# First join: the residual add on GpSimd and one step more of lag; attention: both normalisings of the rows on GpSimd

## What is computed

```python
x = ln(x + rglru_3_layers(x))            # the last step of it is an rmsnorm with a weight
x = ln(x + moe_8_experts_top1(x))
x = ln(x + attention(x))                 # 16 heads; attention ends with (y - mean) / sqrt(var + 1e-3) * gamma + beta
x = ln(x + moe_16_experts_top4(x))
```

## Time and profile before

| | |
|---|---|
| median of 3 runs | 1974.94 us (1974.58 to 1975.36) |
| profiled execution, its own time | 1975.52 us |
| its span, first to last instruction | 1973.8 us |
| busy: PE, DVE, ACT, POOL | 1650.0, 1166.6, 1102.8, 612.8 us |
| mean granted TensorE clock | 0.915 |
| first join, about | 375 to 442 us |
| attention's main loop, about | 870 to 1268 us |

### The profile page before, as it was taken

The page is one execution under the profiler, slowest core; times in us unless marked ns, Lnnn a source line. Parts: engine busy times, 40 slices in busy tenths (PEclk is TensorE's granted clock), DMA queues, the critical chain, the costliest instruction groups (busy, mean ns, idle before and its releaser), DMA issues. The chain is left out here.

```text
span 1973.8 us, 33223 instructions
## 1 busy us (share of the span) xinstructions
PE 1650.0 (84%) x9891; PEld 1114.9 (56%) x9892; DVE 1166.6 (59%) x1942; ACT 1102.8 (56%) x2288; POOL 612.8 (31%) x562
## 2 busy tenths in 40 slices
PE   4999998461599689999999999924999999999990
PEld 1433333260499556444444444522899999999990
DVE  6999997478411164458999999268233333333324
ACT  6888987440133234138888888714455555555554
POOL 0000000000266231211222222110567777777750
PEclk9999999685699889989999999965899999999995
DMA  5000000124122296503334333177344444444417
GB/s 176 1 0 0 0 0 0 49 85 167 33 68 60 66 329 235 87 14 81 77 96 100 99 95 97 40 253 248 61 70 73 67 70 71 67 67 68 70 21 255
DMA packets 145736, 173.68 MB, mean 88 GB/s; under 512 B 29139, under 2 KB 110430, under 8 KB 145504
## 3 DMA queue, kind: packets, MB, share of 16 engines
q1 hardware_dynamic: 104160, 128.29, 21.3%
q0 software_dynamic: 33248, 43.71, 12.5%
q10 hardware_dynamic: 8224, 0.39, 0.2%
HBM read 111.50 MB, written 66.19 MB: 90 GB/s over the span
## 5 line engine op out<-in xcount | busy, mean ns | idle before, releaser
L1312 PEld LDWEIGHTS f_ht_ps<-f_XT,f_WS 128*128 128x128 f32 x2912 | 358.0, 195 | 15.8 <-DVE f_WS L1405 2.6
L1312 PE MATMUL f_ht_ps<-f_XT,f_WS 128*128 128x128 f32 x2912 | 361.8, 278 | 3.0 <-ACT f_XT L1353 3.0
L1320 PE MATMUL f_y_ps<-W,f_HT 128*128 x1456 | 344.1, 379 | 0.0
L2128 DVE TENSOR_REDUCE att_MX<-att_s_ps 128x2 f32<-128x1024 f32 x256 | 304.8, 1215 | 57.6 <-PE att_s_ps L1888 57.5
L1278 POOL DMA_INDIRECT moe<-f_Y,TOK x182 | 276.6, 1520 | 184.8 <-ACT f_Y L1378 122.1
L2093 ACT ACTIVATE att_PT<-att_st_ps 128x512 f32<-128x512 f32 x512 | 278.7, 595 | 53.7 <-PE att_st_ps L1913 46.2
L1320 PEld LDWEIGHTS f_y_ps<-W,f_HT 128*128 128x128 f32 x1456 | 262.8, 190 | 28.3
L1405 DVE COPY f_WS<-W 128x1024 f32 x182 | 133.7, 735 | 209.0 <-PE f_ht_ps L1312 128.0
L1269 POOL DMA_INDIRECT XG<-x,TOK x182 | 191.8, 1054 | 196.1 <-issue 125.9
L1413 DVE TENSOR_TENSOR f_Y<-f_y_ps,f_B 128x256 f32<-128x256 f32 x143 | 60.7, 425 | 292.4 <-PE f_y_ps L1320 292.4
L303 PE MATMUL rec_ring<-rec_XC,rec_W 128*128 128x512 f32 x384 | 181.7, 627 | 51.2 <-DVE rec_XC L353 21.6
(11 more groups left out here) (273 smaller groups left out, 2195.9 us busy)
## 6 DMA issues: line engine op xcount, KB each, us to landing
W<-in_w SPq DMA_DIRECT2D x48, 512.0 KB, 10.0
att_Q<-qk_pairs SPq DMA_DIRECT2D x192, 64.0 KB, 2.8
att_K<-qk_pairs SPq DMA_DIRECT2D x192, 64.0 KB, 2.9
qk_pairs<-prj_HI SPq DMA_DIRECT2D x16, 512.0 KB, 3.8
qk_pairs<-prj_LO SPq DMA_DIRECT2D x16, 512.0 KB, 5.1
hidden<-in_xT SPq DMA_DIRECT2D x8, 512.0 KB, 8.0
x<-n_Y SPq DMA_DIRECT2D x8, 512.0 KB, 3.0
prj_X<-x SPq DMA_DIRECT2D x8, 512.0 KB, 8.8
```

The source lines that it names most:

```text
L1312: mm = nc.tensor.matmul(ht_ps[r % 2][:, f * P:(f + 1) * P], WS[r % 2][:, at:at + P], XT[r % 2][:, c], start=(c == 0), stop=(c == DC - 1))
L1320: mm = nc.tensor.matmul(y_ps[r % 2][:], HT[r % 2][:, f], W2[:, bass.ds(e * W_EXPERT + f * D, D)], start=(f == 0), stop=(f == FC - 1))
L2128: nc.vector.tensor_reduce(MX[n % 2][:, qc, :, p], s_ps[m % 2][:], AX.X, ALU.max).then_inc(s_mx, 1)
```

## The change

In the first join VectorE's `add` is taken apart: `y_scale` (the scaling) and `z_moments` (statistics and aggregates) stay, the add of the residual rows is done by GpSimd, and the steps are spread over one group more. In attention the first normalising of batches 0 to 6 and the second of batches 0 to 5 go from ScalarE to GpSimd, as `tensor_scalar` with multiply and add, all four tiles at once behind the send of the maxima. The constants for ScalarE's slots go.

```diff
-    LAG = 2 if scaled_on_act else 3
+    LAG = 2 if scaled_on_act else 4
...
             st.clear_old(pool)
+            for q in range(GROUPS if rms_w is not None else 0):
+                k = q % N
+                if q >= len(rows):
+                    pool.wait_ge(s_x[k], loads * (q // N + 1))
+                elif q == 0:
+                    pool.wait_ge(rows_loaded, 16 * len(rows))
+                pool.wait_ge(s_y, QT * (q + 1))
+                nc.gpsimd.tensor_tensor(Y[k][:], X[k][:], Y[k][:], ALU.add).then_inc(s_sum, 1)
...
-                if 0 <= step - 1 < GROUPS:
-                    second(step - 1)
+                if 0 <= step - 2 < GROUPS:
+                    second(step - 2)
...
+            def y_scale(q):
...
+                dve.wait_ge(s_rstd1, q + 1)
+                for j in range(QT):
+                    n = QT // 2 * q + j // 2
+                    nc.vector.scalar_tensor_tensor(out=Y[k][:, j], in0=y_ps[n % QT][:, (j % 2) * D:(j % 2 + 1) * D],
+                                                   scalar=rstd1[:, k, j], in1=WB[:], op0=ALU.mult, op1=ALU.mult).then_inc(s_y, 1)
+
+            def z_moments(q):
+                dve.wait_ge(s_sum, q + 1)
+                moments(Y[q % N], stats, mv, q, s_mv)
...
-            for step in range(0 if scaled_on_act else GROUPS + 6):
+            for step in range(0 if scaled_on_act else GROUPS + 7):
                 if 0 <= step - 1 < GROUPS:
-                    add(step - 1)
+                    y_scale(step - 1)
                 if 0 <= step - 2 < GROUPS:
-                    normalise(step - 2)
-                if plus is not None and 0 <= step - 3 < GROUPS:
-                    next_residual(step - 3)
-                if router is not None and 0 <= step - 6 < GROUPS:
-                    copy_logits(step - 6)
+                    z_moments(step - 2)
+                if 0 <= step - 3 < GROUPS:
+                    normalise(step - 3)
+                if router is not None and 0 <= step - 7 < GROUPS:
+                    copy_logits(step - 7)
...
-Y_MOMENTS, Y_ROOT, Y_SHIFT, Y_NORM = KC, KC + 2, KC + 3, KC + 4
-Z_STATS, Z_MOMENTS, Z_ROOT, Z_SHIFT, Z_NORM = 18, 22, 24, 25, 26
+Y_MOMENTS, Y_ROOT, Y_SHIFT = KC, KC + 2, KC + 3
+Z_STATS, Z_MOMENTS, Z_ROOT, Z_SHIFT = 18, 22, 24, 25
...
+            def y_normalise(b):
+                pool.wait_ge(s_yshift, b + 1)
+                for j in range(KC):
+                    nc.gpsimd.tensor_scalar(rows_of(b)[:, j], rows_of(b)[:, j], yrstd[:, b, j], yshift[:, b, j],
+                                            ALU.mult, ALU.add).then_inc(s_yn, 1)
+
+            def z_normalise(b):
...
             for n in range(NGROUPS + 3):
                 if n < NGROUPS:
                     stack_maxima(n)
+                if n % PER == 0 and n >= 2 * PER:
+                    y_normalise(n // PER - 2)
+                if n % PER == 2 and n >= 2 * PER + 2 and n < NGROUPS:
+                    z_normalise(n // PER - 2)
                 if n >= 3:
                     add(n - 3)
...
             def join_step(b, s):
                 if s == Y_ROOT:
                     y_root(b)
-                if Y_NORM <= s < Y_NORM + KC:
-                    y_normalise(b, s - Y_NORM)
                 if s == Z_ROOT:
                     z_root(b)
-                if Z_NORM <= s < Z_NORM + KC:
-                    z_normalise(b, s - Z_NORM)
```

More of the change, by code:

```diff
@@ L707, in minus @@
                 return nc.vector.scalar_tensor_tensor(out=out, in0=mean, scalar=-1.0, in1=scale, op0=ALU.mult, op1=ALU.mult)
+            def y_scale(q):
+                k = q % N
+                if q >= N:
+                    dve.wait_ge(s_rstd, q - N + 1)
+                    dve.wait_ge(s_st[k], 16 * (q // N))
+                    if transposed:
+                        dve.wait_ge(s_zt, DC * (q - N + 1))
+                dve.wait_ge(s_rstd1, q + 1)
[6 more added lines that the diff above has]
+                moments(Y[q % N], stats, mv, q, s_mv)
             def add(q):
                 k = q % N
[L711 to L714, removed]
+                dve.wait_ge(s_x[k], loads * (q // N + 1))
                 if q >= N:
                     dve.wait_ge(s_rstd, q - N + 1)
[L717 to L727, removed]
                 if affine is not None:
@@ L1860, in residual @@
                 nc.gpsimd.tensor_tensor(rows_of(b), rows_of(b), X[b % XS][:], ALU.add).then_inc(s_sum, 1)
+            def y_normalise(b):
[4 more added lines that the diff above has]
+            def z_normalise(b):
+                pool.wait_ge(s_zshift, b + 1)
+                for j in range(KC):
+                    nc.gpsimd.tensor_scalar(rows_of(b)[:, j], rows_of(b)[:, j], zrstd[:, b, j], zshift[:, b, j],
+                                            ALU.mult, ALU.add).then_inc(s_z, 1)
             for k in range(2, STACKS):
```

## The result

The changed kernel takes **1959.49 us** (median of 5 runs, 1958.58 to 1964.03) against 1974.94: a ratio of 0.9923, 95% interval 0.9912 to 0.9934, 15.4 us less, where 10.2 were forecast. It is half a microsecond under the low end of the range. The profiled execution has a span of 1957.8 us.

What follows compares the result with a forecast made beforehand. VectorE was taken to set the pace in the first join, TensorE in attention's main loop. 5.7 us from the join plus 4.5 from attention, 10.2 off 1975.5, gave 1964.7 us off the median; range 1960.0 to 1971.5.

Steps and rivals of the forecast that it cites:

- Rival C: First join: normalising isn't held by GpSimd's add, steps of 4.82, gain 9.0 us, 1961.4 in all; chance 0.05.
- rival B: First join: TensorE's clock at half holds up a step, the join gains only 3.0 us, 1967.4 in all; chance 0.10.
- Normalising stands for 0.65, and runs 1.38: the step is 5.5 us: First join: VectorE's normalising waits 0.65 us for GpSimd's add, so a step falls from 6.03 to 5.5 us.
- I take 0.4 for TensorE's tail: End of the first join: TensorE has one group more behind it, costing 0.4 us of the 6.1 gained.
- I take 0: First join: scaling 1 meeting GpSimd's first add costs nothing, where the bounds were 0 and 1.7 us once.
- 0.10: Attention, group of 11.97: two normalisings leaving ScalarE gain 0.10 us a batch.
- 0.42: Attention, group of 12.83: TensorE's 0.42 us wait behind ScalarE's exponential is gained in each batch.
- 0.25: Attention, group of 12.12: four normalisings leaving ScalarE gain 0.25 us a batch.
- The second stays: Attention, group of 12.83: TensorE's 0.41 us wait behind a VectorE subtraction, slow beside GpSimd's add, remains.
- VectorE's own: Attention: the group of 12.46 is set by VectorE's load, busy 12.36 us, and stays as long.
- Rival A: Attention: ScalarE was never in the way, so only the first join gains, 1969.2 us in all; chance 0.12.
- rival D: Attention: GpSimd is slow at scale-and-shift, beyond 1.1 us an instruction; at 2.39 the kernel slows to 1994 us; chance 0.07.

Runs made afterwards that it cites:

- the kernel with halves: The changed kernel with GpSimd's first-join adds each cut in two of 128x512, each half waiting for its own two scalings; 1955.94 us, ratio 0.9897.
- the kernel with pieces: The changed kernel with GpSimd's multiply by gamma and residual add in attention each cut into four of 128x256; 1953.88 us, ratio 0.9889.
- first_norm_only: The changed kernel with attention's second normalisings of batches 0 to 5 back on ScalarE; 1963.23 us, ratio 0.9933.
- attn_only: Attention as in the changed kernel, the first join as in the kernel before; 1972.71 us, ratio 0.9978.
- vector_adds_spread: The changed kernel with the first join's eight residual adds back on VectorE, the wider spread of the steps kept; 1965.89 us (one run).

## Why the prediction missed, step by step

**The mechanism of the join was right, two of its terms were too dear.** The add left VectorE, normalising was the only thing held, the adds took the 2.35 us of the earlier trace rows, and nothing waited for GpSimd but the first moments, 0.16 us. Rival C (not held) and rival B (clock) both fell: past 405 us, where they came twice before, TensorE's half-clock products came once.

- *"Normalising stands for 0.65, and runs 1.38: the step is 5.5 us"* is the first step that failed. I laid durations end to end. They overlap: in the earlier trace rows a scaling takes 1.65, but in the changed kernel statistics that don't wait for it start 1.57 behind its start, and the four held normalisings run 1.92, not 2.03. The earlier trace rows already showed the second: the normalising there ended 0.14 us behind the add, although four in a row take 1.38 and one about a quarter of that. The step is 5.19. Over six steps that is 1.9 us.
- *"I take 0.4 for TensorE's tail"* is the second. The tail is 1.6 us shorter, not 0.4 longer: 2.0 us. I had read the earlier trace rows as the price of a half clock and had not asked where the kernel before pays it. It pays it a second time at 430.86, in the tail, for a wait that the spreading takes away. The kernel that only spreads has the shorter tail too, which shows it.
- 5.7 + 1.9 + 2.0 = 9.6; measured 9.4.
- The bound for rival C was short in its own terms: with steps of 4.82 the schedule gives 6.1 + 6 x 0.68 = 10.2, less 0.4 for the tail 9.8, not 9.0. With it the low end of the range would have been 1959.5, right at the measured time.
- *"I take 0"* for the scaling that meets the first add held: the scaling of 386.67 ran inside the adds of 386.11 to 390.77 and took 1.66. By the Trainium skill (SBUF — State Buffer, Who interferes with whom), an instruction with one input in SBUF outside the two-port modes doesn't contend; the traces agree, here and in the kernel with halves, where every scaling has an add beside it.

**Attention: 4.5 forecast, 4.2 by the change.** The six batches gave 0.61 each, 3.7 us (0.77 each forecast); the group of the last send gave 0.3 (12.82 to 12.53), and what lies behind it 0.3, so the seventh normalising brought 0.6 and not 0.9. Of the three terms of 0.77, *0.10* for the group of 11.97 was wrong, it didn't move in any kernel; *0.42* measured 0.33, as 0.49 less 0.17 for the dearer meeting, which no term had; *0.25* measured 0.27. That term was right in cause and near in size; what failed beside it is *"The second stays"*: the meeting stayed, but another instruction was held in it. Of the group of 12.46, *"VectorE's own"*, 0.45 was not its own, as the kernel with pieces shows; it stayed all the same. Rival A falls by that (its "VectorE is busy 11.2 to 12.4" should have read 11.0 to 12.4), and rival D by 546 ns, half of its deciding point: GpSimd's gap of 4.39 us had room for 2.16. The further 1.8 us in attention of the profiled execution lie ahead of the third group, with no changed work in them, and are not in the second execution.

**What no step had: the experts' block, 1.3 us.** TensorE's clock, table by stretch, where the first experts' products start; before, then after:

```profile
520.00:525.00 5.00, 4.09 (x18) 3.72 (x19) 0.00 (x0) 0.37 (x1) 3.86 (x4) 0.50 0.35 92
525.00:530.00 5.00, 4.39 (x21) 4.01 (x21) 0.69 (x1) 0.86 (x2) 2.14 (x3) 0.50 0.27 78
530.00:535.00 5.00, 5.00 (x34) 4.69 (x33) 1.39 (x2) 2.19 (x5) 1.29 (x1) 0.96 0.00 0
```
```profile
514.00:519.00 5.00, 4.27 (x19) 3.93 (x20) 0.69 (x1) 0.86 (x2) 3.98 (x4) 0.52 0.38 100
519.00:524.00 5.00, 5.00 (x38) 4.79 (x39) 0.69 (x1) 1.33 (x3) 1.01 (x1) 1.00 0.20 54
```

Before, some 10 us of products ran at 1.2 GHz until the clock was granted in full, after it some 5. It repeats: 240.3 us in three executions with the join of before, 238.3 to 239.2 in nine with a spread join, and once 241.3 (`first_norm_only`). The clock goes with it: counted from the block's first constant, it was granted in full from about 84 us on in these nine, and from about 88 in the other four, `first_norm_only` among them. So the length goes by the clock, and a spread join isn't enough for the earlier one. What decides when the clock comes back is left open, and whether the change causes it is not shown.

The sum for the medians: 9.4 + 4.2 + 1.3 = 14.9 of 15.4 us. That it closes so well is partly luck, since blocks without changed work differ by up to 2 us between executions.

## What to carry to other kernels

Work that moves to GpSimd should be put in pieces when VectorE has instructions that a GpSimd operation holds: the price of a meeting was the rest of the operation less 0.14 to 0.26 us (2.36 left cost 2.21, 0.80 cost 0.54, 0.27 cost 0.13, 0.17 nothing). A quarter of the size made a batch 1.1 us shorter although GpSimd worked 0.4 longer for each whole, but part of that was a new order of the two engines, so look after such a change at what now meets what. When a group takes longer than its engines' work, look into the group before it for a held instruction; a busy engine may be working off a debt. And price the drain behind a loop from its own rows: a half clock there cost its full 1.6 us, while the same in the loop (416.40) cost nothing.

## What the runs showed of the hardware

- GpSimd's multiply and add with two scalars a partition over 128x256 in fp32 takes 546 ns, its two-input operations of that size 726 to 732.
- Four GpSimd operations of 128x256 take 2.80 us, one of 128x1024 2.37; two of 128x512 take 2.51.
- Some VectorE instructions that meet a GpSimd operation with two inputs in SBUF stand until it is nearly or wholly over: the rounding took 2.39 us beside 2.37, against 0.18 alone, the subtraction 2.23, and normalising beside the add lost 0.54. Others run on: four statistics took 1.39 to 1.41 us, aggregates 0.38, and scalings 1.65 or 1.66, beside an add or not.
- The meeting in attention has three outcomes with the same code. The rounding is held (groups of 12.5 us), or the subtraction behind it (12.33), or neither, in one batch of six of `attn_only` and of `vector_adds_spread`: a group of 11.86 or 11.87, and behind it one of 11.99. Then GpSimd is the one that waits, 0.43 us behind the multiply instead of 0.14, after which its add starts in the middle of the subtraction, which takes its 0.18. The last outcome, in attention alone, VectorE and GpSimd:

```profile
1067.88 0.18 DVE L2146 CAST att_MS<-att_MX 128x16 fp32r<-128x16 f32 x1
1068.09 0.18 DVE L2147 TENSOR_TENSOR att_MS<-att_MX,att_MS 128x16 fp32r<-128x16 f32 x1
```
```profile
1065.35 2.38 POOL L1857 TENSOR_TENSOR att_OUT<-att_OUT,att_WB 128x1024 f32<-128x1024 f32 x1
1068.16 2.37 POOL L1860 TENSOR_TENSOR att_OUT<-att_OUT,att_X 128x1024 f32<-128x1024 f32 x1 [0.43 <-POOL att_OUT L1857]
```

In each of the three outcomes the rounding starts within 0.02 us of where the add starts, or would have started, 0.14 us behind the multiply. What decides between them the rows don't tell.
